# Two conditioned attention blocks on one core: means subtracted as aggregated, filler products ahead of two maxima, queues redrawn

## The reference

```
# block 0
xn = ln(x);  q = softmax(xn@Wq+bq over a head);  k = softmax(xn@Wk+bk+mask over time);  v = (xn@Wv+bv)*mask
att = einsum('bnhd,bnhl->bhdl', k, v);  y = einsum('bnhd,bhdl->bnhl', q, att)
scale, shift = split(silu(emb) @ W_emb + b_emb)
x = x + silu(ln(y)*(1+scale)+shift) @ W_out + b_out
# block 1
q, k, v = xn@q_w+q_b, xn@k_w+k_b, (xn@v_w+v_b)*mask
att = softmax(q.k + mask over keys);  y = att.v;  the same end with its own weights
```

## Time and profile before

| | us |
|---|---|
| median of 3 runs (lowest, highest) | 825.99 (822.73, 827.06) |
| profiled execution | 826.59 |
| its span, first to last instruction | 824.9 |
| TensorE busy in it | 797.7 (97%) |
| VectorE busy | 735.6 (89%) |
| ScalarE busy | 704.5 (85%) |
| GpSimd busy | 688.7 (83%) |
| mean granted clock of TensorE, of 1 | 0.989 |

### The profile page before, as it was taken

The page is one execution under the profiler, slowest core; times in us unless marked ns, Lnnn a source line. Parts: engine busy times, 40 slices in busy tenths (PEclk is TensorE's granted clock), DMA queues, the critical chain, the costliest instruction groups (busy, mean ns, idle before and its releaser), DMA issues.

```text
span 824.9 us, 27262 instructions
## 1 busy us (share of the span) xinstructions
PE 797.7 (97%) x9407; PEld 572.0 (69%) x9407; DVE 735.6 (89%) x1488; ACT 704.5 (85%) x1658; POOL 688.7 (83%) x1021
## 2 busy tenths in 40 slices
PE   7998999999999999999999999999999999999995
PEld 3575776777777777677777777777777777666643
DVE  6899999998989999989898889989898989898962
ACT  2366678999898998898898998889989999999995
POOL 8579899999878999789898999888889987896423
PEclk9899999999999999999999999999999999999998
DMA  7522355354344443334545543353454433444411
GB/s 184 153 40 67 96 140 133 81 119 112 86 108 109 105 126 102 98 90 98 122 107 136 121 98 84 84 134 106 110 122 109 109 88 80 99 104 128 116 34 39
DMA packets 149276, 86.11 MB, mean 104 GB/s; under 512 B 87404, under 2 KB 141802, under 8 KB 149130
## 3 DMA queue, kind: packets, MB, share of 16 engines
q1 hardware_dynamic: 149140, 84.36, 42.4%
HBM read 39.64 MB, written 25.80 MB: 79 GB/s over the span
## 4 chain that ended last, share of the span: by engine, by line
PE 41%; issue 12%; POOL 9%; DVE 9%; DMA 2%; SPq 1%; ACT 1%; POOLq 0%; DVEq 0%; ACTq 0%
PE banks L708 11%; PE banks L861 7%; PE banks L716 5%; PE banks L835 4%; PE banks L848 4%; PE banks L723 3%; DVE NM L1308 3%; PE banks L738 2%; PE banks L787 2%; PE banks L871 2%; DVE st L1199 1%; POOL YN L2015 1%; POOL rs L2011 1%; POOL ZHL L2036 1%; POOL SH L2088 1%
## 5 line engine op out<-in xcount | busy, mean ns | idle before, releaser
L1308 DVE TENSOR_REDUCE NM<-banks 128x4 f32<-128x1024 f32 x256 | 306.4, 1212 | 25.1 <-PE banks L835 24.0
L1807 ACT ACTIVATE wraw<-banks 128x1024 f32<-128x1024 f32 x154 | 155.9, 1034 | 8.0 <-PE banks L848 7.3
L2011 POOL TENSOR_TENSOR rs<-ve,nhalf 128x2 f32<-128x2 f32 x128 | 89.7, 703 | 31.6 <-ACT ve L1682 31.4
L1807 ACT ACTIVATE PX<-banks 128x1024 f32<-128x1024 f32 x102 | 103.5, 1035 | 8.6 <-PE banks L848 7.3
L2088 POOL TENSOR_TENSOR SH<-ST,SH 128x512 f16<-128x512 f32 x64 | 74.4, 1164 | 31.4 <-ACT SH L1771 31.4
L708 PE MATMUL banks<-wo,SH 128*128 128x256 f16 x768 | 94.9, 274 | 4.5 <-POOL SH L2088 4.4
L708 PE MATMUL banks<-wv,ZT 128*128 128x256 f16 x768 | 93.5, 273 | 1.4 <-DVE wv L1404 0.5
L835 PE MATMUL banks<-SK,SQ 51*128 51x256 f16 x1024 | 92.5, 272 | 0.8 <-ACT wemb L1815 0.3
L848 PE MATMUL banks<-SQ,SK 53*128 53x256 f16 x1024 | 90.6, 271 | 2.1 <-DVE NM L1308 1.0
L2036 POOL TENSOR_TENSOR ZHL<-Z,ZHL 128x256 f16<-128x256 f32 x128 | 87.5, 704 | 2.6
L861 PE MATMUL banks<-wraw,V 128*32 128x256 f32 x1232 | 87.2, 385 | 0.8 <-DVE NM L1308 0.8
(11 more groups left out here) (186 smaller groups left out, 1879.5 us busy)
## 6 DMA issues: line engine op xcount, KB each, us to landing
scr<-AB SPq DMA_DIRECT2D x64, 256.0 KB, 2.6
X<-in_x_dram SPq DMA_DIRECT2D x32, 256.0 KB, 2.8
SK<-scr SPq DMA_DIRECT2D x64, 128.0 KB, 2.9
SQ<-scr SPq DMA_DIRECT2D x64, 128.0 KB, 2.7
out_dram<-wemb SPq DMA_DIRECT2D x32, 256.0 KB, 2.5
SK<-scr SPq DMA_DIRECT2D x64, 64.0 KB, 2.9
SQ<-scr SPq DMA_DIRECT2D x64, 64.0 KB, 2.7
wemb<-in_L_cond_W_emb_dram SPq DMA_DIRECT2D x1, 1024.0 KB, 5.5
```

Of the source, the lines that this page charges most:

```text
L1308: V.tensor_reduce(NMe[:, c, :, 2 * g:2 * g + 2], banks[:, n:n + 2, :].rearrange("p a (h m) -> p a h m", m=T), AX.X, ALU.max, negate=True). ...
L1807: A.activation(px(v % 5), banks[:, n:n + 2, :].rearrange("p a n -> p (a n)"), ACT.Exp, scale=r_uu).then_inc(S["exp"])
L2011: G.tensor_tensor(rs[:, b % 2, l, :], ve[:, b % 2, l, :], nhalf[:, :], ALU.pow).then_inc(S[f"r{l}"])
```

## The change

1. **Means.** ScalarE no longer copies the means with changed sign (128 instructions go, with their tile `nm`); GpSimd subtracts the mean as bn_aggr wrote it in `mv`. Since GpSimd now reads `mv` itself, bn_aggr of a sequence waits for GpSimd's use two sequences earlier, where it waited for ScalarE's.
2. **Filler products.** `keep_busy` puts products of the zeroed tile, as in `hot`, ahead of a small product: 4 ahead of `tr_w0` and 8 ahead of `ar_o0`, in the bank that the small product will write. `first_part` waits for both once, because it is the first to write the tile.
3. **Order.** The queues of all five engines and the tables BANK and FREED are drawn anew.

```diff
-            def mean_of(b, l):
+            def spread(b, l):
                 k, a = l % 2, (ZS ** -2, 1.0)[l % 2]
...
-                A.activation(nm[:, b % 2, l, :], mv[:, b % 2, l, :, 0], ACT.Copy, scale=-1.0)
                 A.activation(ve[:, b % 2, l, :], mv[:, b % 2, l, :, 1], ACT.Identity, bias=epa[:, k:k + 1],
                              scale=a).then_inc(S[f"n{l}"])
...
             def moments(b, l):
                 e.wait_ge(S[f"s{l}"], b + 1)
-                e.wait_ge(S[f"n{l}"], up(b - 1))
+                e.wait_ge(S[("c0", "yn0", "c1", "yn1")[l]], up(b - 1))
...
-                    i = G.tensor_scalar(dst[:, t, :], src[:, t, :], nm[:, b % 2, l, t:t + 1], rs[:, b % 2, l, t:t + 1], ALU.add, ALU.mult)
+                    i = G.tensor_scalar(dst[:, t, :], src[:, t, :], mv[:, b % 2, l, t, 0:1], rs[:, b % 2, l, t:t + 1],
+                                        ALU.subtract, ALU.mult)
...
+            def keep_busy(g, n):
+                ready(e, "hz")
+                clear(e, g, 0)
+                h = AB[:, 0, 0].rearrange("p a t -> p (a t)")
+                for i in range(n):
+                    PE.matmul(banks[:, home(g), :], h[:, 0:P], h, start=True, stop=True)
+
-            def across(x, of, a, z):
+            def across(x, of, a, z, n=0):
+                keep_busy(f"gt_{x}", n)
                 ready(e, of, "cst")
-                clear(e, f"gt_{x}", 0)
...
-            def spread(x, a, z):
+            def spread(x, a, z, n=0):
+                keep_busy(f"ga_{x}", n)
                 ready(e, f"mx_{x}", "cst")
-                clear(e, f"ga_{x}", 0)
...
-                across("w0", "w0m", 0, 3)
+                across("w0", "w0m", 0, 3, 4)
...
-                spread("o0", 6, 7)
+                spread("o0", 6, 7, 8)
...
-                first(e, b, "fcs", "hot")
+                first(e, b, "fcs", "hot", "tr_w0", "ar_o0")
...
     "gy0T": (
-        "film0 q1:3 f1m ka:2 ka:3 Y0:7 exp:16 exp:23 yt:15 exp:39 at:13 yt:27 Y0:14 Y1:17 yt:39 exp:88 at:19 "
+        "mx_f0 q1:3 qa:1 max:3 ke:7 qa:4 exp:16 yt:11 exp:31 exp:39 at:13 yt:27 at:15 at:16 yt:38 max:100 "
...
-            ld_m(); ld_w0(); x_in(0); x_in(1); ld_r(); ld_o0(); ld_c(); x_in(2); fd(); mbd0(); ld_f0(); z0T(0)
+            x_in(0); ld_m(); ld_w0(); x_in(1); ld_c(); ld_o0(); fd(); x_in(2); ld_r(); fill_k(); mbd0(); ld_f0()
```

More of the change, by code:

```diff
@@ L86 @@
[L86 to L91, removed]
+    "gbb1": "2",
+    "gk0": "02311526326426255650132374540323",
+    "gq0": "24350611637002712141727265651062",
+    "gfx0": "3",
+    "gv0": "24764431145205441163026130464125",
+    "gqt": "35237227436360046223110402512675",
@@ L121 @@
     "gat": (
[L122 to L126 removed]
+        "kt:1 v:2 q1:4 ka:1 at:4 kt:6 kt:7 kt:8 yt:6 qa:6 qa:7 yt:18 yt:22 qa:10 yt:29 exp:69 Y1:19 yt:41 "
@@ L263 @@
     "PE": (
-        "hot pm tr_w0 row3 ar_w0 tr_o0 cnd bb0 ar_o0 bb1 fx0 fm0 tr_f0 ar_f0 tr_w1 ar_w1 rw col tr_b tr_o1 "
-        "ar_b fx1 ar_o1 fm1 tr_f1 bb2 ar_f1 ").split(),
+        "hot cnd pm tr_w0 tr_o0 ar_w0 row3 bb0 ar_o0 bb1 fx0 fm0 tr_f0 tr_w1 ar_f0 ar_w1 rw tr_o1 col tr_b "
+        "ar_b fx1 ar_o1 fm1 bb2 tr_f1 ar_f1 ").split(),
     "DVE": (
-        "hz mb0 w0m mx_w0 o0m csl w0p mx_o0 p3 wl_k0 wl_q0 o0p wl_v0 wl_o0 f0m mx_f0 w1m film0 mx_w1 w1p "
-        "wl_k1 bm o1m mx_b fcs wl_q1 mx_o1 o1p f1m wl_v1 wl_o1 mx_f1 film1 ").split(),
+        "hz mb0 csl w0m o0m mx_w0 w0p mx_o0 p3 wl_k0 wl_q0 o0p wl_v0 wl_o0 f0m w1m mx_f0 film0 mx_w1 w1p o1m "
+        "wl_k1 bm mx_o1 mx_b fcs wl_q1 o1p f1m wl_v1 mx_f1 film1 wl_o1 ").split(),
     "ACT": (
-        "th csT pa wh_k0 wh_q0 wh_v0 bc1 bc0 mc wh_o0 fy0 wh_k1 perm wh_v1 wh_q1 fy1 wh_o1 bc2 ").split(),
+        "th csT mc pa wh_v0 wh_k0 bc0 bc1 wh_q0 wh_o0 fy0 wh_q1 wh_k1 wh_v1 perm fy1 bc2 wh_o1 ").split(),
     "POOL": (
@@ L1044, in col @@
                 t.then_inc(C["PE"])
-            hot(); pm(); tr_w0(); row3(); ar_w0(); tr_o0(); cnd_t(); bb0(); ar_o0(); bb1(); k0(0); q0(0); fx0()
-            v0(0); ktT(0); fm0(); q0(1); att(0); qtT(0); k0(1); tr_f0(); y0(0); v0(1); k0(2); ar_f0(); ktT(1)
-            qtT(1); q0(2); att(1); v0(2); y0T(0); tr_w1(); y0(1); q0(3); v0(3); ar_w1(); k0(3); o0(0); ktT(2); rw()
-            qtT(2); y0T(1); col(); k0(4); att(2); tr_b(); q0(4); tr_o1(); ar_b(); fx1(); ktT(3); y0(2); o0(1)
-            q1p(0); ar_o1(); k1p(0); qtT(3); att(3); ktT(4); fm1(); v0(4); k0(5); y0T(2); tr_f1(); q0(5); y0(3)
@@ L1181, in _ @@
-            pv(30, 3); cols(30, 7); pv(30, 4); ty(30, 0); y1T(29); pv(30, 5); pv(30, 6); o1(28); pv(30, 7)
-            cols(31, 0); cols(31, 1); ty(30, 1); cols(31, 2); pv(31, 0); cols(31, 3); cols(31, 4); pv(31, 1)
-            cols(31, 5); pv(31, 2); cols(31, 6); pv(31, 3); pv(31, 4); cols(31, 7); pv(31, 5); y1T(30); pv(31, 6)
-            pv(31, 7); ty(31, 0); ty(31, 1); o1(29); y1T(31); o1(30); o1(31)
+            hot(); cnd_t(); pm(); tr_w0(); tr_o0(); ar_w0(); row3(); bb0(); ar_o0(); bb1(); k0(0); q0(0); fx0()
```

1002 lines of the change are left out of this document (504 added, 498 removed), and 192 rows, old and new, of the table FREED.

## The result

The changed kernel takes **973.7 us** (median of 4 runs, 971.8 to 975.8) against 826.5 for the kernel before: a ratio of **1.179 [1.174, 1.184]**. The forecast was 820.8 us in a range of 815 to 829. It was wrong in sign and in size: 147 us slower.

What follows compares the result with a forecast made beforehand. VectorE was taken to bound the preparation, TensorE and VectorE the middle, ScalarE the end; -3.0 + 0.3 - 1.0 - 1.2 - 0.3 = -5.2 us from 826.59 gave 821.4, by the median 820.8 us, range 815 to 829.

Steps and rivals of the forecast that it cites:

- Part 4, GpSimd's form: GpSimd's scale-and-shift with a subtraction takes its old 586 ns: 0; at 704 ns at most about +5 us.
- Part 4, the copies: Dropping ScalarE's 128 copies gives -1.2 us near the end and -0.3 in the middle, the latter bounded by 0 and -5.
- Part 5, the redrawn order: Redrawn order of the rest of all queues costs 0; bounds -5 and +13.5 us from VectorE's wait before its maxima.
- Rival 4: VectorE's maxima wait for row products, 0.5 us more in each of 27 sequences: 13.5 us slower, 834.3 us; chance 0.10.
- its threshold of 33: Rival 4 decides once VectorE's idle time before the maxima is over 24 + 9 = 33 us.
- Part 1, the fillers: Twelve fillers ahead of waiting small products cost nothing, hold the clock and remove two VectorE waits: -3.0 us, bounds 0 and -3.0.
- my sign for part 1: Clock at 2.4 GHz from 18 to 30 us, and the reductions of kmr and Q without a wait.
- rival 1: Clock falls all the same, as TensorE idles 2.0 to 2.2 us before k0(0), after bb1: 823.1 us; chance 0.15.
- Parts 2 and 3, the start: Reordered first transfers and VectorE work: +0.3 us; a new bank for y0T(2) near 82 us removes its wait: -1.0 us.
- Rival 3: The start's gain doesn't reach the end, only the end's 1.2 us is left: about 824.8 us; chance 0.15.
- The tests that I named: Forecast wrong if first row products start no earlier than 92.38 us, or the 732 us thereafter change by over 3 us.

Runs made afterwards that it cites:

- e5: The changed kernel with ScalarE's 128 copies back and GpSimd adding them; redrawn order and fillers kept: 885.2 us, 1.070 against the kernel before.
- e1: The changed kernel with GpSimd adding the mean from mv instead of subtracting it (values off by twice the mean): 878.8 us, 1.065.
- e2: The kernel before, in its own order, with ScalarE copying the mean with its own sign and GpSimd subtracting it: 955.6 us, 1.156.
- e3: The kernel before with a different scale-and-shift form in each of a sequence's four normalizations, two of them subtracting: 897.5 us (a single run).
- e4: The kernel before, own order, without the 128 copies; GpSimd adds mv, VectorE's moments have the new wait: 824.1 us, 0.998.
- e13: e5 with one of two HH activations left out of each th0 and th1 from the second sequence on (62 ScalarE instructions): 857.2 us, 1.039.
- e6: e5 without the twelve filler products: 883.3 us, 1.070.
- e11: e5 with VectorE's queue alone drawn again, pieces moved a few places so km and row maxima stand less often behind st0 or st1: 884.8 us, 1.072.
- e7: The kernel before, in its own order, with the change's 4 and 8 filler products alone: 824.4 us, 0.998.
- e8: The kernel before with SyncE's queue of transfers alone taken from the changed kernel: 921.9 us, 1.114.

## Why the prediction was wrong

**Sum.** The loss falls into three steps in a row: +59.6 for order and fillers (e5), -6.4 for the copies (e1), +94.9 for the subtraction. They make 148.1 us over the 825.6 that the kernel before took beside e1 and e5, and 147.2 over the 826.5 beside the changed kernel. In another sequence of steps they would be shared out otherwise: the subtraction alone is +130 (e2).

**Part 4, GpSimd's form: the larger failed term.** The step was: "I take the nearer one, its own, so 0; at 704 it would be ... at most about +5". Measured 1259 and 1229 ns and +95 us (+130 in the old order). Two errors. The bound was taken from the only GpSimd row that subtracts, on two tensors, as if a neighbour in the list were a limit; nothing in the trace showed that a subtraction costs no more than that. And GpSimd's "idle 17%" was taken as cover: 172 us more do not fit in 136 us of idle time (824.9 - 688.7), and of the 172 only 42 were covered in the old order, where they cost 130. In e3 some 86 us more cost 72. At these rates the 30 us would have cost 23 to 25, an estimate, and not 5.

**Part 4, the copies: right as far as can be told.** Forecast -1.5; e4 measured -1.4, new wait included, with 0 to -3.6 in its interval, so that the close hit is partly luck. ScalarE's busy time fell by 8.8 us in e4 (704.5 to 695.7) and by 9.8 from e5 to e1, nearer to the 13 that the 0.09 us between starts gave than to the 28 of the mean. In the redrawn order they were worth 6.4 us, which fits with ScalarE's time being on the path there (e13).

**Part 5, the redrawn order: the second failed term.** "I cost it at 0", with bounds -5 and +13.5; it is +59.6, and the fillers have no measurable part in it (e6). I had compared the distances between steps of TensorE's own queue, which are nearly the same, and bounded the loss by one wait of VectorE, that for the rows. What changed is the order of steps of *different* engines against each other. Rival 4 had the kind right (new waits of VectorE in each sequence), but the wrong instruction and a quarter of the size (13.5 us): the wait before the maxima went from 24.0 to 29.2 us in e5, under its threshold of 33, while that before ST went from 4.0 to 36.2. Which of the new waits make the 59.6 us stays open: ScalarE's time is on the path (e13), yet 20 us less before ST gave nothing (e11). In the changed kernel itself the maxima's wait is 44.4 us, but there GpSimd is the bound.

**Part 1, the fillers: failed too, with little weight.** Forecast -3.0; -1.2 by the medians in the old order (e7), nothing measurable in the new (e6). The step that failed is "they lie in front of instructions that wait anyway". In the old order the eight stand behind the same wait (the row of e7). In the new order there is no such wait any more, and they hold up bb1 and with it wh_q0 (the rows of e5 and e6). The two reductions have no wait of their own in the changed kernel, as my sign for part 1 asked, but the first starts at 29.69 us instead of 26.01, since VectorE waited 3.88 us for ScalarE's wq just ahead of it.

The clock fell all the same, but not where rival 1 put it, in the idle time behind bb1. In the changed kernel it was at half speed from about 15.3 to 25.6 us, and the eight fillers started at 20.15, within that stretch. Between the thirty warming products and the fall TensorE was idle for 0.83, 0.41, 0.37 and 0.79 us, each less than the 1.40 us that had brought no fall. In e5, with the fast form and the same queues, it fell as well (0.72 and 0.77 in the two windows from 10 to 30 us), and in e6 without fillers (0.72 and 0.60); of the four traces in this order only e1 has 1.00 in both. So the fall doesn't come from GpSimd's slow form, and the fillers don't prevent it; what decides it stays open.

**Parts 2 and 3, the start.** The first row maximum of e5 came 0.7 us sooner than before, that of e1 4.8 us sooner (88.0); forecast some 3.7. The sequences behind it lose more than that. Rival 3 (the start's gain doesn't reach the end) can't be judged from these. Against it speaks the kernel before itself: in the 50 executions that ran beside the experiments those with a higher mean granted clock were shorter, 4.6 us for each 0.01 of clock (correlation -0.74, which by itself shows no cause). One hundredth of 825 us is 16.5 us at half clock, so a microsecond at half clock goes with some 0.28 us of time, an estimate; part 1 had 3.0 us for 10.2. The windows from 80 to 100 us of the changed kernel show the clock at 1.00, as forecast, but e1 and e5 have 0.91 there: the fall came a few microseconds later instead (from about 89 and 93 us).

**The tests that I named** were the right ones, and both say that the forecast was wrong. The first row products of the changed kernel start at 98.31 us, not before 92.38. The stretch from there to the end grew from 732 us by 61 in e5 and by 143 in the changed kernel.

## What to carry to other kernels

Price each new operation code by a row of that very code; where the trace has none, let the range hold a doubling, as here, times the count; 256 instructions on an engine busy 83% made that the largest term. Don't cost a redrawn order of five strict queues at 0: compare, for each step that waits, what stands behind it in its queue and who waits for that, across engines and not within one. And before a filler goes in front of a wait, look at what its own first wait is, and at who waits for what stands behind it.

## What the runs showed of the hardware

GpSimd's tensor_scalar on 128x256 float32 takes 1220 to 1259 ns with a subtraction in either place and 557 to 627 ns with addition and multiplication alone, while its tensor_tensor subtraction takes 704 ns. I had expected no difference. And the same instructions on the same engines, only in another order, can be 7% slower with VectorE, ScalarE and GpSimd busy for the same time within some 1% (e5), or 11% by SyncE's list alone (e8). And TensorE's clock fell to 1.2 GHz in the changed kernel though no idle stretch since the warming products was longer than 0.83 us, where the kernel before kept 2.4 GHz over one of 1.40 us.
